# A graph layer's mixing stage: roots moved to VectorE, residual row made by GpSimd, ScalarE's pieces spread out

## The chip, the cores and the metric

The kernel runs on one core of a Trainium2 chip. The metric is the device time of one execution in microseconds (us); lower is better.

## The reference, cut to what matters

```python
xn = layernorm(x)                                   # x: 6250 nodes x 256
gnn = relu(scatter(norm * (xn @ W)[src], dst) + b)  # 200,000 edges
# the mixing layer, over the same nodes
q, k, v = split(xn @ Wqkv.T); q, k = elu(q) + 1, elu(k) + 1     # 8 heads of 32
t  = (q @ sum(k v)) / (q @ sum(k) + 1e-6)
x1 = layer_norm(t + xn) * ln1_g + ln1_b
y  = gelu(x1 @ W1.T + b1) @ W2.T + b2
mix = layer_norm(y + x1) * ln2_g + ln2_b
x = x + gnn + mix
out = x + mixture_of_experts(layernorm(x))          # 8 experts, one per node
```

The change lies in the three lines from `x1` to `mix`. Both layer norms take the root of a variance.

## The kernel before, in words

The 6250 nodes are 49 blocks of 128 rows. After a first stage (products, lists of edges; about 160 us) the second stage walks 74 turns of the graph part, 16 steps to a turn, some 1194 steps in all. On every engine the same order of steps is written out in Python, and each engine's queue runs in that order; semaphores join them.

The graph part of a step: VectorE makes two one-hot tiles (`one_hots`, L1766), two steps ahead of their use (`ONER` is 3 buffers); TensorE multiplies them into `p_b` (`build`, L1139, its semaphore `built` counts steps); ScalarE copies `p_b` to `adj` (`fill`, L1554); TensorE multiplies `adj` with the nodes into `p_m` (`dense`, L1149, 49 products to a turn). `p_b` has two buffers: `build(n)` waits until `fill(n - 2)` has run. Once a turn, `move`, `select`, `combine`, `add` and `start` bring the sums into `acc`. Every second turn takes new edges: GpSimd gathers them by two indirect DMAs (L1087, L1090), VectorE codes them (`code`), TensorE turns them.

The mixing layer is laid over these steps. Steps 0 to 863 carry 780 "halves", 12 to an iteration. The first 13 iterations sum keys and values, 4 blocks each. From then on one iteration is one block: iteration `b` makes the queries of block `b`, normalises block `b - 1` (`norm1`), and carries block `b - 2` through the hidden layer and the output product, and block `b - 3` through the second norm (`norm2`) and the sum (`finish`). A half has a number `k` from 0 to 11, and each engine's `mix_half` says which piece it does at which `k`. One iteration is thus 864 / 65 = 13.3 steps. After step 863 come routing pieces, and then the experts.

The pieces that the change touches, before it:

- TensorE `output` (L1213 to L1218): the product with W2, then `x1T` times the identity (which adds `x1` back, transposed), then a product of a row of ones with `b2`, all into `p_y`.
- ScalarE: `Sqrt` of each variance (`std_y` at k = 2, L1487; `std_t` at k = 4, L1461); at k = 5 one after another `normalised_y` (L1492, reads `p_y`), `gelu` (L1481), and `queries` (`Relu` L1512, `Exp` L1515); `normalised_t` (L1468) at k = 7, `x1_transposed` (L1474) at 9, `x_normalised` (L1499) at 10.
- VectorE: `norm` for each of the two norms, statistics and then five instructions on one number a row (reciprocal L1867, one Newton step L1871 to L1875, L1877).
- GpSimd: only the gathers, as soon as VectorE has coded the group before.

Of the kernel before, what the change touches and what calls it, by code (L numbers as in the profile page):

```python
# [7 lines left out]
ALU = mybir.AluOpType  # L8
# [44 lines left out]
EPS = 1e-5  # L53
EPS_ATTN = 1e-6
# [43 lines left out]
def build(nc, x, srcR, dstR, dstF, gW, gb, WqkvT, ln1g, ln1b, W1T, b1, W2T, b2, ln2g, ln2b, gateW, gateb,  # L98
# [3 lines left out]
    with ExitStack() as top:  # L102
# [56 lines left out]
        bias_b = {k: sb("bc_" + k, [P, C]) for k in ("gb", "ln2g", "ln2b")}  # L159
        b2row = sb("b2row", [1, C])  # L160
# [16 lines left out]
def prepare(nc, sb, ps, sem, g):  # L177
# [21 lines left out]
    with ExitStack() as st:  # L199
# [91 lines left out]
        def _(sp):  # L291
# [12 lines left out]
            for k, v in (("gb", g["gb"]), ("ln2g", g["ln2g"]), ("ln2b", g["ln2b"])):  # L304
# [4 lines left out]
            sp.dma_start(g["b2row"][:], g["b2"].rearrange("(a c) -> a c", a=1)).then_inc(dma_w, 16)  # L309
# [4 lines left out]
            sp.wait_ge(dma_w, 16 * 12)  # L314
# [65 lines left out]
        def _(v):  # L380
# [219 lines left out]
            v.wait_ge(dma_w, 16 * 12)  # L600
# [168 lines left out]
def edges_to_output(nc, sb, ps, sem, g):  # L769
# [9 lines left out]
    NDMA_W = 12  # L779
# [20 lines left out]
    with ExitStack() as st:  # L800
# [9 lines left out]
        mv1, mv2 = work.take("mv1", [P, 2]), work.take("mv2", [P, 2])  # L810
        sd1, sd2 = work.take("sd1", [P, 1]), work.take("sd2", [P, 1])
        r1, r2 = work.take("r1", [P, 1]), work.take("r2", [P, 1])
        nm1, nm2 = work.take("nm1", [P, 1]), work.take("nm2", [P, 1])
        tmp1, tmp2 = work.take("tmp1", [P, 1]), work.take("tmp2", [P, 1])
        x1n = work.take("x1n", [P, C])
        x1T = work.take("x1T", [P, CH, P])
# [23 lines left out]
        lg, cand, cur = work.take("lg", G8), work.take("cand", G8), work.take("cur", G8)  # L840
# [16 lines left out]
        routed.at += 2 * 2 * P * 4  # L857
# [54 lines left out]
        t_mul, t_add, s_st1, var1, std1, n1 = (sem("m_" + n, st) for n in (  # L912
            "tmul", "tadd", "st1", "var1", "std1", "n1"))
        x1n_ok, x1T_ok, gelu_ok = (sem("m_" + n, st) for n in ("x1n", "x1T", "gelu"))
        s_st2, var2, std2, n2, yn_ok, fin = (sem("m_" + n, st) for n in ("st2", "var2", "std2", "n2", "yn", "fin"))
# [125 lines left out]
        def _(sp):  # L1041
            sp.dma_start(g["fb1_sb"][:], g["fb1"]).then_inc(g["dma_fb"], 16)

# [39 lines left out]
        def _(pool):  # L1083
            nc.gpsimd.iota(iota4[:], [[1, P], [0, IB]], 0, 0, allow_small_or_imprecise_dtypes=True).then_inc(iota_ok, 1)
            for q in range(NGRP):
# [6 lines left out]
                                             ).then_inc(edge_rows, 16)  # L1092

# [35 lines left out]
        def _(t_):  # L1129
# [297 lines left out]
        def _(s):  # L1427
# [30 lines left out]
            def std_t(c):  # L1458

                s.wait_ge(var1, c + 1)  # L1460
                nc.scalar.activation(sd1[:], mv1[:, 1:2], ACT.Sqrt, bias=g["eps_ln"][:]).then_inc(std1, 1)  # L1461

            def normalised_t(c):

                s.wait_ge(n1, c * 5 + 5)
                if c > 0:
                    s.wait_ge(built, x1_turned(c - 1))
                nc.scalar.activation(x1n[:], att[:].rearrange("p a c -> p (a c)"), ACT.Identity, scale=r1[:],  # L1468
                                     bias=nm1[:]).then_inc(x1n_ok, 1)
# [14 lines left out]
            def std_y(c):  # L1484

                s.wait_ge(var2, c + 1)
                nc.scalar.activation(sd2[:], mv2[:, 1:2], ACT.Sqrt, bias=g["eps_ln"][:]).then_inc(std2, 1)  # L1487

            def normalised_y(c):

                s.wait_ge(n2, c * 5 + 5)
                nc.scalar.activation(yn[:], p_y[:, 0:C], ACT.Identity, scale=r2[:], bias=nm2[:]  # L1492
# [35 lines left out]
            def mix_half(it, k):  # L1528
# [4 lines left out]
                if k == 2 and 0 <= b - 3 < NBLK:  # L1533
                    std_y(b - 3)
                if k == 4 and 0 <= b - 1 < NBLK:
                    std_t(b - 1)
# [7 lines left out]
                if k == 7 and 0 <= b - 1 < NBLK:  # L1544
                    normalised_t(b - 1)
                if k == 9 and 0 <= b - 1 < NBLK:
                    x1_transposed(b - 1)
                if k == 10 and b + 1 < NBLK:
# [203 lines left out]
        def _(v):  # L1752
# [103 lines left out]
            def norm(b, n, src, ready, made, stt, st_sem, mv, var, sd, std, r, nm, tmp, s_n):  # L1856

                V = nc.vector
                if n == 0:
                    v.wait_ge(ready, made)  # L1860
                    V.bn_stats(stt[:], src).then_inc(st_sem, 1)
                if n == 1:
                    v.wait_ge(st_sem, b + 1)
# [463 lines left out]
```

## Time and the profile before

| | |
|---|---|
| time, median of 3 runs | 2630.99 us (2625.14 to 2633.06) |
| the profiled execution | 2627.53 us, its span 2625.8 us |
| mean granted TensorE clock | 0.923 |
| TensorE busy | 2275.9 us, 87% |
| VectorE busy | 1712.3 us, 65% |
| ScalarE busy | 1362.2 us, 52% |
| GpSimd busy | 281.8 us, 11% |

Busy times are shares of the span; TensorE's matmuls are pipelined and their ends modelled. The clock is a share of 2.4 GHz; it has two levels, 0.5 and 1.0.

### The profile page before, as it was taken

The page shows a single profiled execution, that of the slowest core. Times are in us where ns is not written, and L with a number is a line of the kernel's source. Part 1 is how long each engine was busy: PE and PEld are TensorE (multiplying, and loading weights), DVE is VectorE, ACT ScalarE, POOL GpSimd, SP SyncE. Part 2 cuts the span into 40 slices and gives each one's busy share as a digit, 9 for nine tenths or more (in the row PEclk, how much of TensorE's full clock was granted, in tenths as well). Part 3 has the DMA queues.
Part 4 walks back from the last instruction along what each step waited for, and adds up shares of the span by engine and source line. Part 5 has one row for each costly group of instructions (what it writes and reads, how often), then busy time and mean ns, then how long its engine had stood idle before and what let it go on. Part 6 is the DMA issues. An engine that isn't in the chain of part 4 may idle for free.

```text
span 2625.8 us, 41576 instructions
## 1 busy us (share of the span) xinstructions
PE 2275.9 (87%) x14083; PEld 1625.5 (62%) x14083; DVE 1712.3 (65%) x5505; ACT 1362.2 (52%) x2927; POOL 281.8 (11%) x297
## 2 busy tenths in 40 slices
PE   2749999988898888888888888899998986999998
PEld 2635555666565565565555656666665654899897
DVE  3664444666666666666666766676766665688786
ACT  0345444555655555555555656554444443555563
POOL 7110000000000000000000000000000000243442
PEclk7879999998898988899899989899998988999999
DMA  5000000000000000000000000000111002332230
GB/s 169 9 7 3 3 3 3 3 3 3 3 5 3 3 3 3 3 3 3 3 3 5 3 3 3 3 5 27 37 35 29 33 19 78 97 87 89 63 92 14
DMA packets 51711, 63.21 MB, mean 24 GB/s; under 512 B 15648, under 2 KB 43900, under 8 KB 51378
## 3 DMA queue, kind: packets, MB, share of 16 engines
q1 hardware_dynamic: 26674, 28.66, 3.4%
q0 software_dynamic: 10336, 21.41, 3.0%
q10 hardware_dynamic: 14496, 10.53, 1.2%
q8 instruction: 113, 1.85, 0.3%
q14 instruction: 92, 0.75, 0.1%
HBM read 42.43 MB, written 20.92 MB: 24 GB/s over the span
## 4 chain that ended last, share of the span: by engine, by line
PE 66%; ACT 10%; DVE 9%; issue 6%; DMA 1%; ACTq 1%; POOL 0%; DVEq 0%; another core or an unknown queue 0%; POOLq 0%; SPq 0%
PE p_m L1149 24%; PE p_b L1139 12%; PE p_q L1231 3%; PE p_y L1406 3%; PE p_s L1406 3%; PE p_b L1392 3%; PE p_y L1213 3%; ACT L1481 2%; PE p_s L1160 2%; DVE one_edge L1766 2%; PE p_y L1218 2%; ACT adj L1554 1%; PE p_m L1392 1%; DVE one_src L1766 1%; PE p_nd L1392 1%
## 5 line engine op out<-in xcount | busy, mean ns | idle before, releaser
L1149 PE MATMUL p_m<-node_halves,adj 128*128 128x512 f16 x3626 | 1007.3, 396 | 12.5 <-DVE rows_v L1793 10.9
L1554 ACT CAST adj<-p_b 128x392 f16<-128x392 f32 x1184 | 563.1, 485 | 868.5 <-PE p_b L1139 857.4
L1766 DVE TENSOR_TENSOR one_src<-iota,codes 128x512 bf16<-128x512 bf16 x1184 | 499.0, 421 | 649.5 <-PE p_b L1139 638.8
L1139 PE MATMUL p_b<-one_edge,one_src 128*128 128x98 bf16 x4736 | 613.0, 267 | 164.3 <-ACT adj L1554 155.8
L1139 PEld LDWEIGHTS p_b<-one_edge,one_src 128*128 128x128 bf16 x4736 | 459.5, 117 | 418.7 <-issue 200.6
L1149 PEld LDWEIGHTS p_m<-node_halves,adj 128*128 128x128 f16 x3626 | 363.8, 106 | 249.2 <-issue 54.9
L1766 DVE TENSOR_TENSOR one_edge<-iota,codes 128x392 bf16<-128x392 bf16 x1184 | 421.0, 356 | 0.0
L1087 POOL DMA_INDIRECT src_e<-in_srcR,item_chunk x37 | 37.8, 1021 | 1830.6 <-DVEq L1788 1830.4
L1116 POOL DMA_INDIRECT out_dram<-oo,slot_node x64 | 74.6, 1165 | 220.9 <-DVE oo L2169 202.3
L1231 PE MATMUL p_q<-wq_sb,xnT_m 128*128 128x512 f32 x196 | 97.1, 620 | 0.3 <-ACT xnT_m L1441 0.3
L1098 POOL DMA_INDIRECT rows<-node_features,slot_row x64 | 73.2, 1144 | 165.6 <-DVE slot_node L2276 146.6
L1213 PE MATMUL p_y<-w2t_sb,gT 128*128 128x256 f32 x196 | 79.5, 548 | 0.0
L1160 PE MATMUL p_s<-rows_v,sel 128*128 128x256 f32 x296 | 78.3, 388 | 1.4 <-DVE rows_v L1793 1.4
L2177 DVE TENSOR_TENSOR hTl<-hbuf,hTh 128x978 fp32r<-128x978 f32 x64 | 75.4, 1179 | 2.2
L1406 PE MATMUL p_s<-w2h,hTh 128*128 128x256 f32 x256 | 75.2, 294 | 0.6 <-DVE hTl L2177 0.4
L1406 PE MATMUL p_y<-w2h,hTh 128*128 128x256 f32 x256 | 74.3, 290 | 0.0
L1406 PE MATMUL p_y<-w2h,hTl 128*128 128x256 f32 x256 | 71.9, 281 | 0.0
L1406 PE MATMUL p_s<-w2h,hTl 128*128 128x256 f32 x256 | 71.8, 281 | 0.0
L1406 PE MATMUL p_y<-w2l,hTh 128*128 128x256 f32 x256 | 71.6, 280 | 0.0
L1406 PE MATMUL p_s<-w2l,hTh 128*128 128x256 f32 x256 | 71.6, 280 | 0.0
L1160 PEld LDWEIGHTS p_s<-rows_v,sel 128*128 128x128 f32 x296 | 57.9, 196 | 17.4 <-DVE rows_v L1793 1.8
L1826 DVE TENSOR_TENSOR acc<-acc,p_s 128x256 f32 x148 | 55.4, 416 | 16.1 <-issue 10.7
(345 smaller groups left out, 3697.1 us busy)
## 6 DMA issues: line engine op xcount, KB each, us to landing
w1raw<-in_w SPq DMA_DIRECT2D x8, 1024.0 KB, 5.4
w2raw<-in_w SPq DMA_DIRECT2D x8, 1024.0 KB
res<-in_x SPq DMA_DIRECT2D x7, 896.0 KB, 7.1
node_features<-res ACTq DMA_DIRECT2D x20, 256.0 KB
out_dram<-res ACTq DMA_DIRECT2D x20, 256.0 KB
out_dram<-res SPq DMA_DIRECT2D x1, 1152.0 KB
fb_b<-in_fb SPq DMA_DIRECT2D x1, 1024.0 KB, 9.3
rows<-node_features,slot_row POOLq DMA_INDIRECT x64, 4.1
```

Of the source, the lines that this page charges most:

```text
L1098: nc.gpsimd.indirect_dma_start(rows[0:r, e % 2, t, :], None, feats, bass.IndirectOffsetOnAxis(slot_row[0:r, k:k + 1], 0)).then_inc((gather ...
L1116: nc.gpsimd.indirect_dma_start(out, bass.IndirectOffsetOnAxis(slot_node[0:r, k:k + 1], 0), oo[0:r, t % 2, :], None, bounds_check=N - 1, oo ...
L1139: mm = pe.matmul(p_b[n % 2][:, u * HI2:(u + 1) * HI2], one_src[:, n % ONER, :, u], one_edge[:, n % ONER, :, u], start=True, stop=True)
L1149: mm = pe.matmul(p_m[:], adj[:, k % 2, h, :], node16[:, h, :], start=(h == 0), stop=(h == NBLK - 1))
L1160: mm = pe.matmul(p_s[:, a * C:(a + 1) * C], sel[:, a, :], rows_v[:], start=True, stop=True)
L1213: pe.matmul(p_y[:, 0:C], gT[:, a, :], w2t_sb[:, a, :], start=(a == 0), stop=False, skip_group_check=True)
L1231: pe.matmul(p_kv, xnT[:, a, :], wq_sb[:, a, C:3 * C], start=(a == 0), stop=(a == CH - 1))
L1392: mm = pe.matmul(e_f[c % 4][:, 0:NH[h]], w[:, a, j * P:(j + 1) * P], b[:, a, h * NH[0]:h * NH[0] + NH[h]], start=(q == 0), stop=(q == len( ...
L1406: mm = pe.matmul(e_y[t % 2][:, 0:C], h[:, j, t * P:(t + 1) * P], w[:, j, :], start=(q == 0), stop=(q == len(parts) - 1))
L1554: nc.scalar.copy(adj[:, n // SPV % 2, :, n % SPV * 2 * IB:(n % SPV + 1) * 2 * IB] .rearrange("p h (u r) -> p h u r", r=2), p_b[n % 2][:, 0 ...
L1766: V.tensor_tensor(tile[:, n % ONER], iota4[:, 0:m, :], codes[:, q % 2, a, at:at + IB].rearrange("p (m u) -> p m u", m=1) .broadcast_to([P, ...
L2177: V.tensor_tensor(hTl[:, j, 0:CAPE], hbuf[:, j % NBUF, :], hTh[:, j, 0:CAPE].bitcast(F32), ALU.subtract).then_inc(lo_ok, 1)
```

## The change

Five edits, in all of them only the mixing layer and what it hangs on:

1. TensorE's `output` keeps only the product with W2: four instructions in place of ten for each block (each of its f32 products runs as two). The identity products and the row of ones go.
2. GpSimd makes `x1r = x1n * ln1g + (ln1b + b2)` as a row tile with two 128x256 instructions a block, at k = 9 and 10, and VectorE adds it to `p_y` at the head of `norm2` (result in `yn`, from which the statistics and `normalised_y` read). `ln1g` and `b2` are loaded as broadcast rows (128 KB each, was 1 KB for `b2`), `ln1b` too, at the head of the second stage; GpSimd waits for that load and adds `b2` to it before its first gathers.
3. No `Sqrt` on ScalarE: VectorE makes both roots together, [128, 2] at a time, from a seed by integer arithmetic and three Newton steps, a chain of 12 instructions, six at k = 4 and six at k = 5.
4. ScalarE's pieces are spread: `gelu` and `queries` at k = 5 and 7, in an order that alternates with the parity of the block; `normalised_y` at 6, `normalised_t` at 8, `x1_transposed` at 10, `x_normalised` at 11. TensorE's `output` and `transposes_x1` go from 8 to 9, `attention` from 10 to 11; VectorE's `queries` from 9 to 10, `finish` to 7, 8, 9.
5. GpSimd walks the steps too: the gathers of group q, from q = 2, are issued at step 4 of the odd turn before they are coded, in one order with the new row instructions.

Some tiles of the routing stage (`lg`, `cand`, `cur`) move to other places in the memory.

```diff
-    NDMA_W = 12
+    NDMA_W = 13
-        X_AT, Q_AT, Y_AT, A_AT = 0, 4, 8, 10
+        X_AT, Q_AT, Y_AT, A_AT = 0, 4, 9, 11
+        NEWTON = 2 + 3 * 3 + 1
+        EDGES_AT = 4
...
             sp.dma_start(g["fb1_sb"][:], g["fb1"]).then_inc(g["dma_fb"], 16)
+            sp.dma_start(x1r[:, 1, :], g["ln1b"].rearrange("(a c) -> a c", a=1).broadcast_to([P, C])
+                         ).then_inc(ln1b_in, 16)
...
+            def row_scaled(c):
+                pool.wait_ge(x1n_ok, c + 1)
+                wait(pool, y_sum, c - 1)
+                nc.gpsimd.tensor_tensor(x1r[:, c % 2, :], x1n[:], g["bias_b"]["ln1g"][:], ALU.mult
+                                        ).then_inc(x1_scaled, 1)
+            def row_biased(c):
+                pool.wait_ge(x1_scaled, c + 1)
+                nc.gpsimd.tensor_tensor(x1r[:, c % 2, :], x1r[:, c % 2, :], g["bias_b"]["b2"][:], ALU.add
+                                        ).then_inc(x1_row, 1)
+            def step(s):
+                T, j = divmod(s, SPV)
+                if T % 2 == 1 and j == EDGES_AT and (T + 3) // 2 < NGRP:
+                    edges_of((T + 3) // 2)
...
+            pool.wait_ge(ln1b_in, 16)
+            nc.gpsimd.tensor_tensor(g["bias_b"]["b2"][:], g["bias_b"]["b2"][:], x1r[:, 1, :], ALU.add
+                                    ).then_inc(bias_sum, 1)
+            for q in range(2):
+                edges_of(q)
+            pool.wait_ge(bias_sum, 1)
...
             def output(b):
                 t_.wait_ge(gelu_ok, b * CH + CH)
-                wait(t_, yn_ok, b)
+                wait(t_, y_sum, b)
                 for a in range(CH):
-                    pe.matmul(p_y[:, 0:C], gT[:, a, :], w2t_sb[:, a, :], start=(a == 0), stop=False,
-                              skip_group_check=True)
-                for a in range(CH):
-                    pe.matmul(p_y[:, a * P:(a + 1) * P], x1T[:, a, :], ident[:], start=False, stop=False,
-                              skip_group_check=True)
-                pe.matmul(p_y[:, 0:C], ones_f[0:1, :], g["b2row"][:], start=False, stop=True,
-                          skip_group_check=True)
+                    pe.matmul(p_y[:, 0:C], gT[:, a, :], w2t_sb[:, a, :], start=(a == 0), stop=(a == CH - 1))
...
-            def std_t(c):
-                s.wait_ge(var1, c + 1)
-                nc.scalar.activation(sd1[:], mv1[:, 1:2], ACT.Sqrt, bias=g["eps_ln"][:]).then_inc(std1, 1)
...
-                s.wait_ge(n1, c * 5 + 5)
+                s.wait_ge(roots, c * NEWTON + NEWTON)
...
-                if k == 5:
-                    if 0 <= b - 3 < NBLK:
-                        normalised_y(b - 3)
-                    if 0 <= b - 2 < NBLK:
-                        gelu(b - 2)
-                    if b < NBLK:
-                        queries(b)
+                if k == 5 + 2 * (b % 2) and 0 <= b - 2 < NBLK:
+                    gelu(b - 2)
+                if k == 7 - 2 * (b % 2) and b < NBLK:
+                    queries(b)
+                if k == 6 and 0 <= b - 3 < NBLK:
+                    normalised_y(b - 3)
...
+            def norm2(b, n):
+                if n == 0:
+                    v.wait_ge(built, output_made(b))
+                    v.wait_ge(x1_row, b + 1)
+                    wait(v, fin, 3 * b)
+                    V.tensor_tensor(yn[:], p_y[:, 0:C], x1r[:, b % 2, :], ALU.add).then_inc(y_sum, 1)
+                    v.wait_ge(y_sum, b + 1)
+                    V.bn_stats(st2[:], yn[:]).then_inc(s_st2, 1)
+            def both_roots(it, i):
+                if i == 0:
+                    v.wait_ge(var1, min(c + 1, NBLK))
+                    wait(v, var2, c - 1)
+                else:
+                    v.wait_ge(roots, c * NEWTON + i)
+                if i == 0:
+                    V.tensor_scalar(w, var, EPS, None, ALU.add).then_inc(roots, 1)
+                elif i == 1:
+                    V.tensor_scalar(r.bitcast(I32), w.bitcast(I32), -0.5, SEED, ALU.mult, ALU.add
+                                    ).then_inc(roots, 1)
...
+                if 0 <= b - 1 < NBLK + 2:
+                    for i in range(NEWTON):
+                        if k == 4 + i // 6:
+                            both_roots(it, i)
```

## Rows read from the trace of the kernel before

**Rows 1.** Windows: busy us (instructions) of PE, PEld, DVE, ACT, POOL, then PEclk.
```profile
500.30:1670.00 1169.70, 1017.73 (x6304) 699.46 (x6302) 777.64 (x2786) 684.78 (x1402) 40.05 (x40) 0.92 0.01 3
...
1700.00:1800.00 100.00, 96.26 (x647) 64.83 (x646) 76.82 (x259) 51.37 (x110) 4.38 (x4) 1.00 0.03 9
```

**Rows 2.** Line L1506, once a mixing iteration: ns min/median/max, first and last start.
```profile
L1506 ACT COPY xnT_m<-p_t x49: 378/379/405, 500.3 to 1669.6; 128x256 f32<-128x256 f32 x49
```

**Rows 3.** Waits between 500.3 and 1670 us: total, times, longest.
```profile
PE p_b L1139 <- ACT adj L1554: 129.1, 57, 4.5
...
PE p_nd L1191 <- DVE kf L1832: 14.4, 17, 1.5
...
PE p_m L1149 <- DVE rows_v L1793: 5.3, 14, 1.2
```

**Rows 4.** Timeline of PE around the longest wait: start, us, what.
```profile
1089.51 0.52 PE L1139 MATMUL p_b<-one_edge,one_src 128*128 128x98 bf16 x4 [3.33 <-ACT adj L1554]
```

**Rows 5.** Windows of 2 us there, columns as Rows 1.
```profile
1086.00:1088.00 2.00, 0.18 (x1) 0.00 (x0) 1.89 (x9) 1.97 (x5) 0.00 (x0) 1.00 0.00 0
...
1092.00:1094.00 2.00, 2.00 (x6) 0.88 (x6) 0.02 (x1) 0.00 (x0) 0.00 (x0) 0.50 0.04 8
```

**Rows 6.** Timeline of ACT in one iteration.
```profile
1058.66 1.28 ACT L1481 ACT_TABLE_LOAD   x1
...
1060.87 1.28 ACT L1515 ACT_TABLE_LOAD   x1
...
1062.16 0.42 ACT L1515 ACTIVATE ke<-ke 128x256 f32<-128x256 f32 x1
```

**Rows 7.** Groups by line, PE and ACT, 500.3 to 1670 us.
```profile
L1216 PE MATMUL p_y<-ident,x1T 128*128 128x128 f32 x184 | 38.8, 351 | 0.0
...
L1218 PE MATMUL p_y<-b2row,ones_f 1*128 1x256 f32 x92 | 40.6, 528 | 0.0
...
L1461 ACT ACTIVATE sd<-mv,eps_ln 128x1 f32<-128x1 f32 x47 | 13.8, 295 | 41.9 <-DVE mv L1864 39.5 <-issue 2.1
```

**Rows 8.** Timeline of PE in an iteration at full clock.
```profile
1043.26 0.61 PE L1216 MATMUL p_y<-ident,x1T 128*128 128x128 f32 x4
1043.80 0.69 PE L1218 MATMUL p_y<-b2row,ones_f 1*128 1x256 f32 x2
```

**Rows 9.** Groups by line, DVE, 500.3 to 1670 us.
```profile
L1766 DVE TENSOR_TENSOR one_src<-iota,codes 128x512 bf16<-128x512 bf16 x639 | 268.6, 420 | 338.9 <-PE p_b L1139 334.5 <-issue 0.7
L1766 DVE TENSOR_TENSOR one_edge<-iota,codes 128x392 bf16<-128x392 bf16 x639 | 227.2, 355 | 0.0
L1826 DVE TENSOR_TENSOR acc<-acc,p_s 128x256 f32 x80 | 30.0, 416 | 5.7 <-issue 5.6
...
L1793 DVE TENSOR_TENSOR rows_v<-rows_v,p_m 128x256 f32<-128x256 f32 x40 | 16.8, 420 | 24.2 <-ACT rows_v L1562 21.8
```

**Rows 10.** Timeline of DVE, two links of a chain.
```profile
1057.29 0.15 DVE L1873 SCALAR_TENSOR_TENSOR tmp<-tmp,r 128x1 f32<-128x1 f32 x1
1057.48 0.16 DVE L1875 SCALAR_TENSOR_TENSOR r<-tmp,r 128x1 f32<-128x1 f32 x1
```

**Rows 11.** Timeline at the head of the second stage.
```profile
160.19 0.35 SPq L1042 DMA_DIRECT2D fb_sb<-in_fb  x1
...
161.57 0.97 POOL L1087 DMA_INDIRECT src_e<-in_srcR,item_chunk  x1 [0.16 <-issue]
...
166.98 0.66 PE L1168 MATMUL p_s<-ident,code_e 128*128 128x128 f32 x2 [19.80 <-DVE code_e L1786]
```

**Rows 12.** DMA issues: KB each, median us to landing.
```profile
fb_sb<-in_fb SPq DMA_DIRECT2D x1, 32.0 KB, 1.7
...
gw_sb<-in_gW SPq DMA_DIRECT2D x1, 256.0 KB, 5.4
```

**Rows 13.** Groups of POOL, whole span.
```profile
L344 POOL TENSOR_SCALAR_AFFINE_SELECT headmask<-headmask 128x128 f32<-128x128 f32 x1 | 2.1, 2052 | 0.1
...
L337 POOL TENSOR_SCALAR_AFFINE_SELECT next_p<-next_p 128x128 f32<-128x128 f32 x1 | 0.3, 293 | 0.1
```

More of the change, by code:

```diff
@@ L158, in build @@
         wq_sb = sb("wq_sb", [P, CH, 3 * C])
[L159 to L160 removed]
+        bias_b = {k: sb("bc_" + k, [P, C]) for k in ("gb", "ln2g", "ln2b", "ln1g", "b2")}
         cols = {k: sb("col_" + k, [P, CH]) for k in ("b1", "ln1g", "ln1b")}
@@ L809, in edges_to_output @@
         st1, st2 = work.take("st1", [P, 6]), work.take("st2", [P, 6])
[L810 to L814, printed above, removed]
+        mv = work.take("mv12", [P, 2, 2])
+        ve, tmp12, r12, nm12 = (work.take(n, [P, 2]) for n in ("ve12", "tmp12", "r12", "nm12"))
         x1n = work.take("x1n", [P, C])
+        x1r = work.take("x1r", [P, 2, C])
         x1T = work.take("x1T", [P, CH, P])
@@ L911, in edges_to_output @@
             "xn", "xnT", "qrel", "qexp", "qT", "den"))
-        t_mul, t_add, s_st1, var1, std1, n1 = (sem("m_" + n, st) for n in (
-            "tmul", "tadd", "st1", "var1", "std1", "n1"))
+        t_mul, t_add, s_st1, var1, roots = (sem("m_" + n, st) for n in (
+            "tmul", "tadd", "st1", "var1", "roots"))
         x1n_ok, x1T_ok, gelu_ok = (sem("m_" + n, st) for n in ("x1n", "x1T", "gelu"))
-        s_st2, var2, std2, n2, yn_ok, fin = (sem("m_" + n, st) for n in ("st2", "var2", "std2", "n2", "yn", "fin"))
+        s_st2, var2, yn_ok, fin = (sem("m_" + n, st) for n in ("st2", "var2", "yn", "fin"))
+        ln1b_in, bias_sum, x1_scaled, x1_row, y_sum = (sem("m_" + n, st) for n in (
+            "ln1b", "biassum", "x1scaled", "x1row", "ysum"))
         (lg_ok, mean_ps, centred, x2_ok, var_ok, std, cols_ok, turned, xT_ok, l_ps, dv, bn_ok, e_ok, e_act,
@@ L1084, in _, with edges_of @@
             nc.gpsimd.iota(iota4[:], [[1, P], [0, IB]], 0, 0, allow_small_or_imprecise_dtypes=True).then_inc(iota_ok, 1)
-            for q in range(NGRP):
+            def edges_of(q):
                 wait(pool, coded_rows, q)
@@ L1092, in _ @@
                                              ).then_inc(edge_rows, 16)
+            def row_scaled(c):
[11 more added lines that the diff above has]
+                    edges_of((T + 3) // 2)
+                for q in halves_at(s):
+                    it, k = divmod(q, PER)
+                    c = it - first_mix - 1
+                    if k == 9 and 0 <= c < NBLK:
+                        row_scaled(c)
+                    if k == 10 and 0 <= c < NBLK:
+                        row_biased(c)
+            pool.wait_ge(ln1b_in, 16)
[4 more added lines that the diff above has]
+            pool.wait_ge(bias_sum, 1)
+            for n in range(LASTSTEP):
+                step(n)
             def load_rows(e):
@@ L1482, in gelu @@
                                          ).then_inc(gelu_ok, 1)
-            def std_y(c):
-                s.wait_ge(var2, c + 1)
-                nc.scalar.activation(sd2[:], mv2[:, 1:2], ACT.Sqrt, bias=g["eps_ln"][:]).then_inc(std2, 1)
             def normalised_y(c):
-                s.wait_ge(n2, c * 5 + 5)
-                nc.scalar.activation(yn[:], p_y[:, 0:C], ACT.Identity, scale=r2[:], bias=nm2[:]
+                s.wait_ge(roots, (c + 2) * NEWTON + NEWTON)
+                nc.scalar.activation(yn[:], yn[:], ACT.Identity, scale=r12[:, 1:2], bias=nm12[:, 1:2]
                                      ).then_inc(yn_ok, 1)
@@ new lines, in both_roots @@
+            def both_roots(it, i):
+                c = it - first_mix - 1
+                lo, hi = (0 if c < NBLK else 1), (2 if c >= 2 else 1)
+                var, r, t, w = mv[:, lo:hi, 1], r12[:, lo:hi], tmp12[:, lo:hi], ve[:, lo:hi]
+                if i == 0:
[8 more added lines that the diff above has]
+                                    ).then_inc(roots, 1)
+                elif i == NEWTON - 1:
+                    V.scalar_tensor_tensor(nm12[:, lo:hi], mv[:, lo:hi, 0], -1.0, r, ALU.mult, ALU.mult
+                                           ).then_inc(roots, 1)
+                elif i % 3 == 2:
+                    V.tensor_tensor(t, w, r, ALU.mult).then_inc(roots, 1)
+                elif i % 3 == 0:
+                    V.scalar_tensor_tensor(t, t, -0.5, r, ALU.mult, ALU.mult).then_inc(roots, 1)
+                else:
+                    V.scalar_tensor_tensor(r, t, 1.5, r, ALU.add, ALU.mult).then_inc(roots, 1)
@@ L1932, in mix_half @@
                             attention(b - 1, n)
-                    for n, at in enumerate((3, 3, 5, 5, 6, 6, 6)):
+                    for n, at in enumerate((3, 3)):
                         if k == at:
```

65 lines of the change are left out of this document (24 added, 41 removed).

## The prediction, made before the changed kernel was seen

> **What bounds the kernel now.** I read the page first: TensorE is busy for 87% of the span, its clock granted at 0.92, so it is the engine to ask about. The number of graph steps is fixed and the change touches only those that carry the mixing layer, so I then took windows by stage [rows 1]. From 500.3 us, when the first block of the mixing is turned, to 1670 us, TensorE is busy for 1017.7 of 1169.7 us (87%) at a clock of 0.92; behind it, in the plain graph turns at 1700 us, it is busy for 96% at 1.00. The mixing stretch thus holds idle time and slow clock that the graph part by itself hasn't. Its unit is an iteration: line L1506 runs once in each, 49 times from 500.3 to 1669.6 us [rows 2], so one takes (1669.6 - 500.3) / 48 = 24.36 us, of which TensorE is busy 1017.7 / 48.02 = 21.19 us and idle 3.17.
>
> The waits say what ends the idle time [rows 3]: 129.1 us, 2.69 an iteration, in 57 waits of up to 4.5 us, is `build` waiting for ScalarE's `fill`; 0.30 is attention for VectorE, 0.11 the turn's sum. ScalarE is only 59% busy [rows 1], so it is not short of time but late in places. Its timeline shows where [rows 6]: at k = 5 `normalised_y`, a table load of 1.28 us, both pieces of `gelu`, `Relu`, a second load of 1.28 and `Exp` stand in one step; from the first load to the end of `Exp` are 62.58 - 58.66 = 3.9 us, with `normalised_y` ahead of it some 4.5, in which no `fill` runs, with only two buffers of `p_b`. The third load and two `Sqrt` stand at k = 2 and 4.
>
> The wait has a tail. At 1086 to 1088 us TensorE did almost nothing, its wait ended at 1089.5 [rows 4], and in the window from 1092 it is busy all the time at a granted clock of 0.50 [rows 5], which is 1.2 instead of 2.4 GHz. By the Trainium skill ("TensorE: Matmul & The Clock Gate", Part 1: The HAM clock gate) the throttled clock is the default and activity releases it; by that rule shorter waits give the clock back too, and the trace agrees here: 1.00 where TensorE is 96% busy [rows 1].
>
> **The change part by part**, per iteration.
>
> TensorE's products: L1216 and L1218 are busy 38.8 + 40.6 us over 46 blocks [rows 7], 1.72 us a block. At full clock they take 43.80 + 0.69 - 43.26 = 1.23 us [rows 8]; the rest is that they stand right behind the long wait, at half clock. Saved: 1.72.
>
> The clock: lost are (1 - 0.92) x 24.36 = 1.95 us at most (part of it is idle time anyway), of which 1.72 - 1.23 = 0.49 is in the 1.72. Of the 1.46 left I take 0.5, a third, since some waits stay and part of the slow time is idle time; the ends are 0 (the clock stays as it is) and 1.46. So TensorE's work is 21.19 - 1.72 - 0.5 = 18.97 us.
>
> ScalarE: two of three table loads (2 x 1.28) and two `Sqrt` (2 x 0.30, [rows 7]) go, 3.16 us, and the wait of `std_t` for VectorE (41.9 / 47 = 0.89) with them. As the order of `gelu` and `queries` alternates, one load an iteration is left. The longest piece without a `fill` is now `Relu` (taken as long as `Exp`), load and `Exp` at k = 7, 0.42 + 1.28 + 0.42 = 2.1 us [rows 6] in place of 4.5. A step takes 24.36 / 13.3 = 1.8 us now and some 1.5 after, and `build` tolerates a lateness of about one. I take 0.4 us of wait for `fill` in place of 2.69; the ends are 0 and 1.7 (2.69 x 2.1 / 4.5 is 1.3, and 0.4 for the roots that ScalarE then waits for at k = 6).
>
> VectorE: idle ahead of L1766 and L1826 for (338.9 + 5.7) / 48 = 7.2 us [rows 9], so occupied for 17.2, of which the wait for ScalarE's half of `move`, some 0.5, can move: 16.7. It gains the 128x256 addition from `p_y`, 0.42 as L1826, and 12 chained small instructions for 10. A link of such a chain takes 57.48 - 57.29 = 0.19 us [rows 10], so 0.38. The integer seed is priced as one more link. Sum 17.5 us, under TensorE's 19.0 but near. It is crowded at k = 1 to 5: the 12 links (2.3 us), five passes over 128x256 (attention, its addition, the new one, two statistics, 0.42 each by L1826) and five small pieces at 0.19 make 5.3 us; 5.5 pairs of one-hots at 0.42 + 0.36 = 0.78 [rows 9] are 4.3; of the turn's some six passes 0.8 falls there: 10.4 us, where TensorE takes 18.97 x 5.5 / 13.3 = 7.8. The 2.6 us of lateness stands against a lead of two steps less a pair, 2 x 1.5 - 0.78 = 2.2. So a new wait, TensorE for one-hots: 0.4 by this, 0.7 taken, since the turn's work falls unevenly; ends 0 and 1.7.
>
> GpSimd: the trace of before has no arithmetic on two tiles on that engine. The nearest rows are a select on 128x128 of 0.29 us and the dearest one of 2.05 [rows 13]; twice the elements and a second input make 3 x 0.29 = 0.87 us each, ends 0.3 and 2.05. Both are made a period ahead of `norm2` (k = 10 of one iteration to k = 1 of the second after, some 25 us), so as work they cost nothing; without that cover `norm2` would wait 1.7 us. The gathers lie 25 steps ahead of `code`, queued only behind these two: nothing. By the Trainium skill ("GPSIMD Engine Reference", 3.1 Elementwise) such an instruction takes about 2.6 cycles of 1.2 GHz an element, an estimate of 0.56 us for 256 and dispatch on top; no run before shows it.
>
> Moved pieces: `output`, `transposes_x1` and `attention` each keep one half between them and what they read; `x_normalised` has one half (some 1.6 us) to `transposes_x` where it had two, and is one short piece: nothing, and up to 0.5 if ScalarE is late there. The other waits (0.48) stay.
>
> New iteration: 18.97 + 0.4 + 0.7 + 0.48 = 20.55 us, 3.81 less. There are 49 blocks: 186.7 us.
>
> The head of the second stage loses. TensorE waits for the first codes there, 19.8 us, and the chain goes through GpSimd's first gather at 161.57 [rows 11]. That now stands behind the load of `ln1b`, the second that SP issues (about 160.5), and an addition. A load of 32 KB landed in 1.7 us, one of 256 in 5.4 [rows 12]; with 0.3 to 2.05 for the addition the gather starts at 162.5 to 168. I take 164.1: +2.5 us, ends 1 and 6.5. The two broadcasts more in the first stage lie ahead of waits that end on other work: nothing.
>
> **The sum**, against the profiled execution: 2627.53 - 186.7 + 2.5 = 2443.3. The median shown stands 3.5 us above it: 2447.
>
> **The rivals.**
>
> A. The forecast, 2447; with the ends of clock, ScalarE and one-hots partly added, 2400 to 2500. Chance 0.60.
>
> B. VectorE and GpSimd hold each other up. VectorE's one-hots read two tiles at once and come every step, 639 pairs in the stretch [rows 9]; where a row instruction of GpSimd runs beside them VectorE stands still for as long: 2 x 0.87 = 1.74 us, and as VectorE is nearly the bound, all of it shows. Period 22.3, gain 2.07 x 49 = 101: 2532. Against it: at k = 9 and 10 VectorE has little to do. Chance 0.12. By the Trainium skill ("SBUF — State Buffer", Who interferes with whom) a VectorE instruction with two inputs in that memory contends with a GpSimd instruction that reads it, and one blocks for the whole of the other; by that rule the case is real, and no run before shows it.
>
> C. All waits but 0.48 go, and 1.0 us of the clock comes back: 21.19 - 1.72 - 1.0 + 0.48 = 18.95, gain 5.41 x 49 = 265: 2369. For it: the 96% at 1.00 with VectorE at 77% [rows 1]. Against it: VectorE's 17.5 in 18.95. Chance 0.10.
>
> D. Slower: a row instruction of GpSimd is far dearer than any row shows and VectorE stands for both. It decides from (24.36 - 17.5) / 2 = 3.4 us each. At 4 us VectorE needs 25.5, +1.14 x 49 = 56: 2690. Against it: twice the dearest row. Chance 0.06.
>
> E. The spreading doesn't do what it says: ScalarE, waiting for the 12-link chain at k = 6 and loading at k = 7, is as late as before, and only the products go, 1.72 x 49 = 84: 2549. For it: 57 waits are about one an iteration, and one load an iteration stays. Chance 0.12.
>
> **How the numbers follow.** The range 2385 to 2555 takes in A with its tails, B and E, and leaves out C and D, 0.16; A's own range stands beside it above. What a measurement of this kernel can tell from no change is about 0.3%, 7.9 us; B, C and E all lie beyond it on the fast side. Faster is A, B, C and E, 0.94, less a hundredth that lies between E and D: 0.93; within 0.3% that hundredth; slower D, 0.06.
>
> **What would show it.** L1506's copies 20.5 us apart; one table load an iteration, about 98 fewer; TensorE's wait for `adj` from 129 us to some 20 to 40, one of a length under 2; a new wait for the one-hots of some 30 us; the mixing's clock at 0.96 or more; 294 matmuls fewer; the first gather at 164 us. Wrong would be: VectorE's one-hots longer than 420 ns beside GpSimd (B, D), a clock still at 0.92, or waits for `adj` near 2.7 us an iteration (E).

## The result, and the profile after

The changed kernel takes 2458.36 us (median of 4; 2454.8 to 2463.17) beside 2628.06 for the kernel before: a ratio of 0.9354, 95% interval 0.9328 to 0.9381, 169.7 us less. The forecast was 2447 us, 184 less. The profile is of the shortest of the four executions, 2454.8 us.

The unit is the mixing iteration again. The line once in each iteration (L1506 before [rows 2], L1531 after) and the windows over just these 48 iterations:

```profile
L1531 ACT COPY xnT_m<-p_t x49: 378/380/405, 502.7 to 1501.4; 128x256 f32<-128x256 f32 x49
```

```profile
502.70:1501.40 998.70, 903.91 (x6024) 624.06 (x6023) 831.65 (x2934) 542.87 (x1216) 121.28 (x134) 0.98 0.01 4
```

An iteration takes (1501.4 - 502.7) / 48 = 20.81 us where it took 24.36. TensorE is busy for 903.91 / 48 = 18.83 of it and idle for 1.98; before it was 21.19 and 3.17 [rows 1]. The granted clock of the stretch went from 0.92 to 0.98. Outside the stretch little moved: the span fell by 2625.8 - 2453.0 = 172.8 us, of which the 48 iterations are 1169.3 - 998.7 = 170.6.

The waits of the stretch (total, times, longest), for [rows 3]:

```profile
ACT yn L1517 <- DVE nm L1914: 52.8, 43, 3.1
...
PE p_nd L1231 <- DVE kf L1852: 27.8, 30, 2.6
...
PE p_y L1253 <- ACT gT L1511: 17.7, 17, 1.6
PE p_t L1238 <- ACT x1n L1498: 16.3, 15, 1.4
...
PE p_b L1179 <- ACT adj L1574: 13.3, 24, 1.5
...
PE p_m L1189 <- DVE rows_v L1813: 8.0, 15, 1.5
PE p_b L1179 <- DVE one_edge L1786: 4.5, 6, 1.1
```

The wait for `adj` fell from 129.1 to 13.3 us, and no wait of it is longer than 1.5 us. In its place stand shorter ones that before had been small or absent: attention for VectorE (27.8, before 14.4), the output product for `gelu` (17.7, before none), and `transposes_x1` for `x1n` (16.3, before 1.2). ScalarE itself now waits 52.8 us, 1.1 an iteration, for the roots. That wait isn't new, it has moved: before, `std_t` waited 39.5 us for VectorE [rows 7], which the prediction took as gone.

The two waits for ScalarE take turns. In TensorE's timeline of two iterations that follow each other:

```profile
984.51 1.13 PE L1253 MATMUL p_y<-w2t_sb,gT 128*128 128x256 f32 x4 [1.32 <-ACT gT L1511]
...
985.48 0.38 PE L1238 MATMUL p_t<-ident,x1n 128*128 128x128 f32 x2
...
1003.76 1.07 PE L1253 MATMUL p_y<-w2t_sb,gT 128*128 128x256 f32 x4
...
1006.21 0.44 PE L1238 MATMUL p_t<-ident,x1n 128*128 128x128 f32 x2 [1.38 <-ACT x1n L1498]
```

Where `gelu` stands at k = 7 TensorE waits for `gT`, and where `queries` with its table load stands there TensorE waits for `x1n`, made at k = 8: whichever piece is at k = 7 sets the wait.

The groups by line of ScalarE and GpSimd in the stretch, for [rows 7, 13]:

```profile
L1511 ACT ACT_TABLE_LOAD x24 | 30.8, 1283 | 0.4
...
L1540 ACT ACT_TABLE_LOAD x23 | 29.5, 1283 | 0.4
```

```profile
L1103 POOL TENSOR_TENSOR x1r<-x1n,bc_ln1g 128x256 f32<-128x256 f32 x47 | 43.3, 921 | 814.0 <-ACT x1n L1498 814.0
L1109 POOL TENSOR_TENSOR x1r<-x1r,bc_b 128x256 f32<-128x256 f32 x47 | 37.1, 790 | 3.6
```

One table load an iteration, and 0.92 and 0.79 us for GpSimd's two instructions. VectorE feels them. Its groups, for [rows 9], and its timeline beside GpSimd's:

```profile
L1786 DVE TENSOR_TENSOR one_src<-iota,codes 128x512 bf16<-128x512 bf16 x639 | 273.2, 428 | 128.0 <-PE p_b L1179 124.3 <-issue 1.0
L1786 DVE TENSOR_TENSOR one_edge<-iota,codes 128x392 bf16<-128x392 bf16 x639 | 234.7, 367 | 0.0
...
L1935 DVE SCALAR_TENSOR_TENSOR res<-res,sqd,yn 128x256 f32<-128x256 f32 x45 | 28.8, 640 | 0.3 <-DVE code_e L1806 0.3
```

```profile
1006.38 0.88 DVE L1786 TENSOR_TENSOR one_edge<-iota,codes 128x392 bf16<-128x392 bf16 x1
1007.19 0.95 DVE L1935 SCALAR_TENSOR_TENSOR res<-res,sqd,yn 128x256 f32<-128x256 f32 x1
```

```profile
1006.23 0.81 POOL L1103 TENSOR_TENSOR x1r<-x1n,bc_ln1g 128x256 f32<-128x256 f32 x1 [8.08 <-ACT x1n L1498]
1007.12 0.73 POOL L1109 TENSOR_TENSOR x1r<-x1r,bc_b 128x256 f32<-128x256 f32 x1
```

A one-hot of 0.36 us takes 0.88 and a pass of 0.48 takes 0.95 where they start just behind one of GpSimd's: each ends 0.2 to 0.3 us after it. By the Trainium skill ("SBUF — State Buffer", Who interferes with whom) a VectorE instruction with two inputs in that memory contends with a GpSimd instruction that reads it, for a port that only one of them can hold. The trace agrees: the two lose 0.52 and 0.47 us of the 0.66 us that they run beside GpSimd's.

The head of the second stage, for [rows 11]:

```profile
163.35 0.72 POOL L1126 TENSOR_TENSOR bc_b<-bc_b,x1r 128x256 f32<-128x256 f32 x1 [2.20 <-DMA x1r<-in_ln1b]
164.23 0.98 POOL L1092 DMA_INDIRECT src_e<-in_srcR,item_chunk  x1
...
169.57 0.66 PE L1208 MATMUL p_s<-ident,code_e 128*128 128x128 f32 x2 [22.65 <-DVE code_e L1806]
```

The first codes reach TensorE at 169.57 in place of 166.98 us, 2.6 later.

### The profile page after: what moved, and what is told of

It is laid out like the page before. It is cut to its first block and busy times, and to the rows that moved or that the text cites. A ratio compares the mean times of both kernels' runs of the same rounds, so it can differ in the third digit from the quotient of the medians.

```text
span 2453.0 us, 41210 instructions
## 1 busy us (share of the span) xinstructions
PE 2157.4 (88%) x13789; PEld 1545.6 (63%) x13789; DVE 1770.2 (72%) x5676; ACT 1213.4 (49%) x2731; POOL 366.4 (15%) x396
## 5 line engine op out<-in xcount | busy, mean ns | idle before, releaser
L1189 PE MATMUL p_m<-node_halves,adj 128*128 128x512 f16 x3626 | 986.5, 389 | 17.1 <-DVE rows_v L1813 14.2
L1574 ACT CAST adj<-p_b 128x392 f16<-128x392 f32 x1184 | 570.0, 485 | 843.0 <-PE p_b L1179 827.7
L1786 DVE TENSOR_TENSOR one_edge<-iota,codes 128x392 bf16<-128x392 bf16 x1184 | 429.0, 362 | 0.0
L1103 POOL TENSOR_TENSOR x1r<-x1n,bc_ln1g 128x256 f32<-128x256 f32 x49 | 44.9, 916 | 840.1 <-ACT x1n L1498 840.1
L1253 PE MATMUL p_y<-w2t_sb,gT 128*128 128x256 f32 x196 | 56.0, 410 | 17.9 <-ACT gT L1511 17.7
```

The lines of the kernel that those rows point to most:

```text
L1189: mm = pe.matmul(p_m[:], adj[:, k % 2, h, :], node16[:, h, :], start=(h == 0), stop=(h == NBLK - 1))
L1574: nc.scalar.copy(adj[:, n // SPV % 2, :, n % SPV * 2 * IB:(n % SPV + 1) * 2 * IB] .rearrange("p h (u r) -> p h u r", r=2), p_b[n % 2][:, 0 ...
L1786: V.tensor_tensor(tile[:, n % ONER], iota4[:, 0:m, :], codes[:, q % 2, a, at:at + IB].rearrange("p (m u) -> p m u", m=1) .broadcast_to([P, ...
```

## The experiments

The kernels ran in three groups of four, each beside runs of the kernel before on the same chip. That kernel took 2634.5, 2627.3 and, for the last group, on a third chip, 2582.0 us. In the traces of that group GpSimd's first instruction of the second stage starts at 111.67 us where it was 159.95, and the first block of the mixing is turned at about 452 us where it was 502: the first stage is about 50 us shorter, with nothing changed in it. I therefore compare the gain over the kernel before of the same group, in us, and the length of an iteration, and give the ratio with its interval. The changed kernel: gain 169.7, iteration 20.81. By the intervals of the ratios, a difference of less than some 8 us between the changed kernel and a run of the first two groups isn't clear of noise by the times alone. The length of an iteration is from one execution of each kernel.

**Which part brings the gain.** First the spread and the roots, without the row:

```diff
-                    pe.matmul(p_y[:, 0:C], gT[:, a, :], w2t_sb[:, a, :], start=(a == 0), stop=(a == CH - 1))
+                    pe.matmul(p_y[:, 0:C], gT[:, a, :], w2t_sb[:, a, :], start=(a == 0), stop=False,
+                              skip_group_check=True)
+                for a in range(CH):
+                    pe.matmul(p_y[:, a * P:(a + 1) * P], x1T[:, a, :], ident[:], start=False, stop=False,
+                              skip_group_check=True)
+                pe.matmul(p_y[:, 0:C], ones_f[0:1, :], g["bias_b"]["b2"][0:1, :], start=False, stop=True,
+                          skip_group_check=True)
...
-                    V.tensor_tensor(yn[:], p_y[:, 0:C], x1r[:, b % 2, :], ALU.add).then_inc(y_sum, 1)
-                    if k == 9 and 0 <= c < NBLK:
-                        row_scaled(c)
-                    if k == 10 and 0 <= c < NBLK:
-                        row_biased(c)
```

> The changed kernel with TensorE's identity and bias products kept and no residual row, no second addition on VectorE, no work of GpSimd but the gathers (ScalarE's spread, the roots on VectorE stay; b2 is read from its broadcast row). Theory (the waits and the clock are most of the gain, and the products cost only their full-clock time once the clock is back): the products come back at 1.23 us an iteration against 0.42 saved on VectorE, so 1.1 us an iteration more than the changed kernel, less 2.6 for the head of the stage: about 2510 us, clock of the mixing still 0.97 or more. Rival (the products are half of the gain): 84 us less gain, about 2542.

Measured: 2475.05 us, ratio 0.9395 (0.9374 to 0.9416), gain 159.5; iteration 21.11. Both theories miss: they allowed some 1.1 us an iteration, or 84 us. Putting the products back costs only 10 us. Its windows, over the 48 iterations:

```profile
501.20:1514.70 1013.50, 953.66 (x6301) 666.73 (x6299) 787.87 (x2889) 541.64 (x1216) 40.90 (x40) 0.99 0.01 4
```

TensorE's work is 19.87 us an iteration, 1.04 more than in the changed kernel, as the theory has it; but its idle time is 1.25 in place of 1.98. The row saves 1.04 us of work and 0.73 of it, 35.0 us in all, comes back as waiting. Two of this run's waits show where most of it is:

```profile
PE p_nd L1222 <- DVE kf L1849: 15.2, 20, 1.5
...
PE p_t L1229 <- ACT x1n L1494: 1.2, 4, 0.3
```

With the row the wait for attention is 12.6 us longer and that for `x1n` 15.1. The six products stand between the product with W2 and `transposes_x1`; while TensorE ran them, `x1n` came. Without them TensorE arrives earlier and waits. That reading is from the two traces; no run moved those products alone. Attention's part a later run took apart.

Then the row alone, on the kernel before (its `output`, `norm2` and GpSimd part as in the change, GpSimd's pieces at k = 8 and 9; `Sqrt`, three loads and ScalarE's order as before):

```diff
+                    V.tensor_tensor(yn[:], p_y[:, 0:C], x1r[:, b % 2, :], ALU.add).then_inc(y_sum, 1)
-                norm(b, n, p_y[:, 0:C], built, output_made(b), st2, s_st2, mv2, var2, sd2, std2, r2, nm2, tmp2, n2)
+                norm(b, n, yn[:], y_sum, b + 1, st2, s_st2, mv2, var2, sd2, std2, r2, nm2, tmp2, n2)
```

> The kernel before with the residual row alone: GpSimd makes it at k = 8 and 9, VectorE adds it, TensorE's six products a block are gone; Sqrt, the three table loads and ScalarE's order stay. Theory: 1.23 to 1.72 us an iteration saved on TensorE, the long wait for ScalarE as it was, since that is not in TensorE's time: 60 to 84 us less 3 for the head, about 2558 us, clock of the mixing still about 0.92. Rival (ScalarE sets the pace around k = 5, so what TensorE saves turns into a longer wait): under 40 us, 2590 or more, with the wait for adj above 2.7 us an iteration.

Measured: 2575.24 us, ratio 0.9769 (0.9752 to 0.9785), gain 59.3; iteration 23.20. The theory holds, at the low end of it: TensorE's work is 949.48 / 48 = 19.78 us an iteration, 1.41 less than before, and its idle time 3.42, 0.25 more. The long wait and the clock are those of before, 133.4 us and 0.92:

```profile
PE p_b L1179 <- ACT adj L1589: 133.4, 54, 4.5
```

```profile
502.90:1616.60 1113.70, 949.48 (x6025) 650.90 (x6023) 832.98 (x2830) 685.60 (x1401) 113.29 (x134) 0.92 0.01 3
```

The two parts alone gain 159.5 and 59.3, together 169.7, not 218.8.

**What in ScalarE's part counts.** Two loads an iteration at the same spread:

```diff
-                if k == 5 + 2 * (b % 2) and 0 <= b - 2 < NBLK:
+                if k == 5 and 0 <= b - 2 < NBLK:
                     gelu(b - 2)
-                if k == 7 - 2 * (b % 2) and b < NBLK:
+                if k == 7 and b < NBLK:
                     queries(b)
```

> The changed kernel with gelu always at k = 5 and queries always at k = 7: the same spread, but two table loads an iteration in place of one. Theory (the longest piece without a fill counts, not the number of loads): the pieces are 1.9 and 2.1 us, none longer than before; some 0.3 us an iteration more, 2465 to 2480 us. Rival (each load costs its 1.28 us): 1.28 x 48 = 61 us more, 2520.

Measured: 2469.36 us, ratio 0.9364 (0.9348 to 0.938), gain 165.2; iteration 21.09. The theory holds and the rival's 61 us are far off. Of TensorE's waits in the 48 iterations the one for `gT` is gone, since `gelu` is never at k = 7, and the one for `x1n` has more than doubled, since `queries` always is. ScalarE waits only 13.9 us for the roots here and is late all the same, by its own load:

```profile
PE p_t L1238 <- ACT x1n L1498: 37.4, 34, 1.7
```

And one load, but in one step:

```diff
-                if k == 5 + 2 * (b % 2) and 0 <= b - 2 < NBLK:
-                    gelu(b - 2)
-                if k == 7 - 2 * (b % 2) and b < NBLK:
-                    queries(b)
-                if k == 6 and 0 <= b - 3 < NBLK:
-                    normalised_y(b - 3)
+                if k == 6:
+                    if 0 <= b - 3 < NBLK:
+                        normalised_y(b - 3)
+                    for i in range(2):
+                        if i == b % 2 and 0 <= b - 2 < NBLK:
+                            gelu(b - 2)
+                        if i != b % 2 and b < NBLK:
+                            queries(b)
```

> The changed kernel with normalised_y, gelu and queries all at k = 6, in the alternating order: still one table load an iteration, but in one piece of 0.6 + 0.6 + 0.4 + 1.28 + 0.42 = 3.3 us after the wait for the roots. Theory (the length of the piece counts): TensorE waits some 1.5 us an iteration for adj again and the clock falls with it, about 2530 us. Rival (the number of loads counts): within 10 us of the changed kernel, about 2462.

Measured: 2538.37 us, ratio 0.9624 (0.9608 to 0.964), gain 96.2; iteration 22.58.

```profile
PE p_b L1179 <- ACT adj L1576: 98.6, 49, 4.2
```

```profile
504.50:1588.50 1084.00, 941.28 (x6025) 645.16 (x6023) 848.51 (x2934) 547.57 (x1216) 113.83 (x134) 0.94 0.01 3
```

Doubling the loads cost 4.5 us of gain by the times, within noise, and 13 by the iterations; putting the pieces in one step cost 73.5, though ScalarE's busy time is nearly the same in it as in the changed kernel (547.57 and 542.87 us). The wait for `adj` is there again, 2.05 us an iteration, and the clock is down to 0.94: wait and clock move together, and 0.78 us of TensorE's busy time come with them (941.28 / 48 = 19.61 against 18.83, the same instructions). This trace is of the longest execution of its kernel, 2548.51 us, 10 above the median; its wait and its iteration are that much on the high side.

**Where the row's gain went.** GpSimd's row work cut to one column from the third block on; this leaves that work out, so later blocks add an older row:

```diff
-                nc.gpsimd.tensor_tensor(x1r[:, c % 2, :], x1n[:], g["bias_b"]["ln1g"][:], ALU.mult
+                w = C if c < 2 else 1
+                nc.gpsimd.tensor_tensor(x1r[:, c % 2, 0:w], x1n[:, 0:w], g["bias_b"]["ln1g"][:, 0:w], ALU.mult
...
-                nc.gpsimd.tensor_tensor(x1r[:, c % 2, :], x1r[:, c % 2, :], g["bias_b"]["b2"][:], ALU.add
+                nc.gpsimd.tensor_tensor(x1r[:, c % 2, 0:w], x1r[:, c % 2, 0:w], g["bias_b"]["b2"][:, 0:w], ALU.add
```

> The changed kernel with GpSimd's two row instructions cut to one column from the third block on, so that every later block adds the row of an earlier one: leaves out the row's work, keeps all semaphores and VectorE's addition. Theory (VectorE and GpSimd block each other, and that is part of what the row costs): VectorE's instructions fall back to their old durations, 24 us less of them over the mixing, and since TensorE waits for VectorE only in places, about half of it shows: 8 to 15 us less than the changed kernel. Rival 1 (the blocking falls where VectorE has slack): within 3 us. Rival 2 (the whole give-back of 0.7 us an iteration is blocking): 30 us less.

Measured: 2449.44 us, ratio 0.9323 (0.9306 to 0.934), gain 177.8; iteration 20.56. VectorE's groups between 505 and 1480 us and a wait of the 48 iterations:

```profile
L1788 DVE TENSOR_TENSOR one_edge<-iota,codes 128x392 bf16<-128x392 bf16 x630 | 224.7, 357 | 0.0
L1937 DVE SCALAR_TENSOR_TENSOR res<-res,sqd,yn 128x256 f32<-128x256 f32 x44 | 21.1, 479 | 0.3 <-DVE code_e L1808 0.3
```

```profile
PE p_nd L1233 <- DVE kf L1854: 15.7, 22, 1.5
```

The durations of before are back (357 and 479 ns), VectorE's busy time fell by 831.65 - 806.57 = 25.1 us. In the kernel's time 8 us of it show, or 12 by the iterations: attention's wait went from 27.8 to 15.7 us, back to what it was without the row (15.2), and the waits for `gT` and `x1n` are unchanged to the tenth (17.7 and 16.3). The blocking is real, and a third to a half of what it takes reaches the time; the intervals of the two times just overlap, so it rests on the trace more than on them.

Two Newton steps in place of three:

```diff
-        NEWTON = 2 + 3 * 3 + 1
+        NEWTON = 2 + 2 * 3 + 1
```

> The changed kernel with two Newton steps in place of three: a chain of 9 instructions, six at k = 4 and three at k = 5 (the roots are less exact). Theory (the chain's length at k = 4 and 5 makes VectorE late, and ScalarE waits 52.8 us for it at k = 6, which passes on to TensorE's waits for gT and x1n): 0.58 us an iteration less on VectorE, ScalarE's wait for nm down to 25 to 35 us, 8 to 20 us less in all. Rival (VectorE's lateness doesn't reach TensorE): under 4 us.

Measured: 2436.87 us, ratio 0.9272 (0.9255 to 0.9289), gain 190.4; iteration 20.41. 20.7 us more gain than the changed kernel, at the top of what the theory gave. ScalarE's wait for the roots is 29.5 us in place of 52.8, TensorE's for `x1n` 10.3 in place of 16.3, for `adj` 7.0 in place of 13.3 and for `gT` 14.8 in place of 17.7; attention's is the same, 27.9:

```profile
ACT yn L1517 <- DVE nm L1914: 29.5, 31, 2.5
```

The head:

```diff
+            edges_of(0)
             pool.wait_ge(ln1b_in, 16)
...
-            for q in range(2):
-                edges_of(q)
+            edges_of(1)
```

> The changed kernel with GpSimd's first gathers ahead of its wait for ln1b and its addition to b2. Theory (the head of the stage lost 2.6 us to that wait): the first codes on TensorE 2.5 us earlier, 2.5 us less in all, at the edge of what can be measured but plain in the trace. Rival (the next wait, for the first products of the keys, takes its place): the codes earlier, the first block of the mixing no earlier.

Measured: 2459.21 us, ratio 0.9363 (0.9345 to 0.9381), gain 168.0; iteration 20.90. In the trace the head came back: from GpSimd's first instruction of the stage to the first codes on TensorE it takes 167.58 - 160.89 = 6.7 us, against 169.57 - 159.95 = 9.6 in the changed kernel, and the first block of the mixing is turned at 499.5 in place of 502.7. The time shows nothing of it, and 2.5 us is less than these times can show. The iterations of that execution are 0.09 us longer, 4.6 us in all, of which 4.5 are TensorE's busy time (908.42 us against 903.91) with the waits the same: the same instructions ran slower. Executions of one kernel differ by that much: the changed kernel's four have mean granted clocks of 0.954 and 0.955 at 2454.8 and 2455.6 us, and 0.950 at 2461.1 and 2463.2.

`normalised_y` moved away from the roots, and `finish`, which reads it, behind it:

```diff
-                if k == 6 and 0 <= b - 3 < NBLK:
+                if k == 9 and 0 <= b - 3 < NBLK:
                     normalised_y(b - 3)
...
-                    for n, at in enumerate((7, 8, 9)):
+                    for n, at in enumerate((10, 11, 11)):
                         if k == at:
                             finish(b - 3, n)
```

> The changed kernel with normalised_y at k = 9 in place of 6 and finish at 10, 11, 11, so that ScalarE doesn't stand for the roots while fill, gelu, queries and x1n are behind it. Theory (the wait at k = 6, 1.1 us an iteration, is what makes x1n and gT late for TensorE): the waits for gT and x1n, 34 us, mostly go, 15 to 30 us less than the changed kernel. Rival (the lateness only moves to k = 9 and 10, ahead of x1T and the next block): within 5 us.

Measured: 2432.04 us, ratio 0.926 (0.9239 to 0.9281), gain 195.2; iteration 20.39. Its waits:

```profile
PE p_nd L1231 <- DVE kf L1852: 39.3, 41, 2.6
...
PE p_y L1253 <- ACT gT L1511: 5.9, 14, 1.6
...
PE p_t L1238 <- ACT x1n L1498: 4.2, 10, 1.2
```

ScalarE's wait for the roots is gone, those for gT and x1n are 10 us in place of 34, and what is left is attention, 39.3 us. That one is VectorE's `queries`, which the change had moved from k = 9 to 10, while attention went from 10 to 11: one half before TensorE wants it, then as now. Back at 9 it has two:

```diff
-                if k == 10 and b < NBLK:
+                if k == 9 and b < NBLK:
                     queries(b)
```

> normalised_y at k = 9 and finish at 10, 11, 11, as in the last run of that kind, and VectorE's queries back from k = 10 to 9. Theory (with normalised_y out of the way the largest wait left on TensorE is attention for VectorE's queries, 39.3 us, because one half is too short for a VectorE that is late): most of it goes, 15 to 30 us less than with queries at 10, about 2410 us. Rival (VectorE itself is near its bound and the wait reappears as one for one-hots or rows_v): within 6 us, about 2430.

Measured (the third chip from here on): 2341.74 us, ratio 0.9064 (0.9044 to 0.9084), gain 240.3; iteration 19.54.

```profile
L1531 ACT COPY xnT_m<-p_t x49: 378/380/406, 452.2 to 1389.9; 128x256 f32<-128x256 f32 x49
```

```profile
PE p_nd L1231 <- DVE kf L1852: 3.4, 6, 1.6
```

The wait went and nothing took its place: 45 us more gain where I had expected 15 to 30. Over the 48 iterations it is 40.8 us, 30.4 of them TensorE's idle time and 10.4 its busy time (892.81 us in place of 903.24 for the same instructions, at 0.99 in place of 0.98): the expectation had no term for the clock. Then with two Newton steps as well:

> The same with two Newton steps. Theory: after normalised_y has moved, nothing waits for the roots, so the three links are worth only their 0.58 us of VectorE where it is late: 5 to 12 us less than with three. Rival (VectorE is the bound): the whole 28 us.

Measured: 2331.68 us, ratio 0.9031 (0.9019 to 0.9043), gain 250.3; iteration 19.27: 10 us less, as expected, where the same step was worth 20.7 in the changed kernel's order. And the second of `gelu` and `queries` at k = 6:

```diff
-                if k == 5 + 2 * (b % 2) and 0 <= b - 2 < NBLK:
+                if k == 5 + b % 2 and 0 <= b - 2 < NBLK:
                     gelu(b - 2)
-                if k == 7 - 2 * (b % 2) and b < NBLK:
+                if k == 6 - b % 2 and b < NBLK:
                     queries(b)
```

> The same with two Newton steps and the second of gelu and queries at k = 6 in place of 7. Theory (gT and x1n have only one half before TensorE wants them, and together they still cost 10 us): the pieces then stand one behind the other, a lateness of some 1.3 us that has two halves to be made good: within 8 us either way. Rival (two pieces in neighbouring halves make ScalarE late for fill again): 10 to 20 us more.

Measured: 2325.13 us, ratio 0.8999 (0.8983 to 0.9014), gain 256.9; iteration 19.23, 0.04 less, which is 2 of the 6.6 us that it gained. The theory holds: with nothing at k = 7 TensorE no longer waits for `gT` or `x1n` (6.3 and 4.9 us in the run before), and waits 10.3 us for `adj` in place of 4.1. This is the fastest version, 87 us more gain than the changed kernel. Last, the row's worth in this order: the first experiment again, with `queries` at 9 and two Newton steps, to be held against the run with the row and two Newton steps.

> The spread and the roots alone (identity and bias products kept on TensorE, no row, normalised_y at k = 6 since p_y must be free for the next output), with queries at 9 and two Newton steps. Theory (with VectorE's lateness cured, TensorE is the bound and its 1.04 us an iteration of products shows in full): 40 us or more slower than the same with the row. Rival (the row gives back on VectorE what it takes off TensorE whatever the order): within 15 us.

Measured: 2384.63 us, ratio 0.9237 (0.9223 to 0.9251), gain 197.4; iteration 20.38. The windows of the 48 iterations, with the row (two Newton steps) and without:

```profile
454.50:1379.60 925.10, 887.49 (x6024) 624.16 (x6023) 802.41 (x2793) 543.90 (x1217) 116.49 (x134) 0.99 0.01 4
```

```profile
449.90:1428.00 978.10, 943.60 (x6301) 664.70 (x6299) 768.37 (x2748) 542.31 (x1216) 40.98 (x40) 0.99 0.01 4
```

TensorE is idle for 0.78 us an iteration with the row and 0.72 without, so the 1.17 us of work that the row saves (18.49 against 19.66) show in full: 53 us, where in the changed kernel's order they had shown as 10. In this pair the row also has `normalised_y` at k = 9, which it allows, since `p_y` is free once the sum is in `yn`; without the row the next `output` would wait for it.

## Why the prediction was right, and what it sized wrongly

**The bound and the mechanism** were right. The long wait for `fill` and the slow clock behind it were most of the time to be had, the length of ScalarE's longest piece sets it (in one step: 73.5 us lost; a second load: 4.5 by the times, 13 by the iterations), and the products on TensorE were the smaller part.

**TensorE's work**: 18.97 us forecast, 18.83 measured. Its two parts missed in opposite directions. The products were put at 1.72; taken off the kernel before, with its clock still at 0.92, they gave 1.41 (the row alone), and at full clock 1.04 to 1.17 in place of 1.23. The clock was then put at 0.5; from the row alone to the changed kernel the same instructions take 19.78 - 18.83 = 0.95 us less.

**Wait for `adj`**: 0.4 forecast, 13.3 / 48 = 0.28 measured. **For one-hots**: 0.7 forecast, 0.12 measured (4.5 us for `one_edge` and 1.3 for `one_src`). VectorE was occupied for 20.81 - (128.0 + 4.3) / 48 = 18.05 us where 17.5 were forecast, the difference being the blocking of 25.1 / 47 = 0.53, but its lead on the one-hots covered that.

**The moved pieces** are the term that was mis-sized. The prediction put down nothing for them and left 0.48 us for all other waits. Measured are 0.58 (attention), 0.37 (gT), 0.34 (x1n) and 0.17 (rows_v), 1.46 us together. Two things were overlooked.

- The distances weren't all kept, as the prediction has it for `output` and the others. Before, `gelu` was at k = 5 and `output` at 8, three halves; in the changed kernel every other block has `gelu` at 7 and `output` at 9, two halves. `normalised_t`, which makes `x1n`, is one half ahead of its use as before; but it had stood two halves behind the table loads of k = 5, and now in every other iteration it stands one half behind the load at k = 7. The waits take turns with the parity of the block, go over wholly to `x1n` with two loads, and are both gone when nothing is at k = 7.
- The engine ahead had become late. VectorE's crowd at k = 1 to 5 didn't hit the one-hots, it hit the roots, which ScalarE then waits for at k = 6 in its one queue, and behind that stand `gelu`, `queries` and x1n. Moving `normalised_y` away showed it (25 us), then giving `queries` a second half (45 us). Attention's wait doubled with its distance unchanged, and the run without the row's work shows 12 us of it to be the blocking.

A sum over the four terms gives 18.83 + 0.28 + 0.12 + 1.46 = 20.69 of the 20.81.

**How near the total came is in part luck.** Against the 20.55 forecast the moved pieces are 0.98 us too low, and the one-hots 0.58, TensorE's work 0.14 and `adj` 0.12 too high, so that 0.84 of the 0.98 cancel.

**GpSimd**: 0.87 us each taken, 0.92 and 0.79 measured. The blocking (B) happened, and the prediction's own sign of it with it (one-hots longer than 420 ns beside GpSimd), though not as a bound: 25 us on VectorE, 8 to 12 in the time, where B had 85 in the time.

**The head**: 2.5 us forecast, 2.6 in the trace.

E, that only the products would count, was wrong the other way round: they were worth 59 us alone and 10 on top of the rest. C, with all waits but 0.48 us gone and an iteration of 18.95, was not reached by the changed kernel; the last order tried comes near it with 19.23. D didn't come near.

What stays open: how much of the 170 us is clock and how much wait, since every run that moved the long wait moved both; and what the row costs through `x1n`, which is read from two traces and no run took apart.

## What to carry to other kernels

When several engines run one written-out order, look for the longest stretch in one queue without the piece that the bounding engine waits for, not at that engine's busy share: the same busy time cost 73 us more when it stood in one step. After such a fix, list every wait of the bounding engine again, down to the small ones, and ask which queue is late behind which wait; moving one piece by three halves and another by one gave 70 us that no operation had to be saved for. When pieces move, write down for each one what it reads, its distance to the reader before and after, and what long piece stands just ahead of it in its own queue. The worth of work taken off the bounding engine depends on that order too: the same row was worth 10 us in one and 53 in the other (with the later place of `normalised_y` that it allows), so a part tried alone, or in a bad order, can't be judged by its time.

## What the runs showed of the hardware that was not expected

GpSimd's 128x256 instruction on two tiles of the on-chip memory takes 0.72 us alone and 0.79 to 0.92 on average beside VectorE, and VectorE's instruction with two inputs in that memory, begun just behind it, goes from 0.36 to 0.88 or from 0.48 to 0.95 us. Cutting GpSimd's work to one column brought both back to their old means.

The granted clock of TensorE over the mixing was 0.92 with waits of up to 4.5 us for `adj`, 0.94 with up to 4.2, and 0.98 to 0.99 in every run whose longest wait for `adj` was 1.5 us or less, though other waits there, for attention, are up to 2.7 us long. The same instructions of TensorE took 19.61 us an iteration at 0.94 and 18.83 at 0.98.
